# A fused six-layer decoder on one core: the step order of four compute engines is laid out anew

## What is computed

```python
x = LN(x + causal_self_attention(LN'(x)) + x)          # one head of 256, float32
x = LN(x + long_convolution(x, k, skip, ctx, ctx))      # 16 heads of 8, via FFT in the reference
x = LN(x + ternary_ffn(x))                              # hidden 1024, quantised to 8 bits, tanh for silu
x = LN(x + recurrence(x))                               # r, k, v, decayed cumulative sum, group norm
x = LN(x + cross_attention(x, ctx, mask))               # 16 heads of 128, 4 key/value heads
x = LN(x + gated_ffn_fp8(x))                            # gelu(x Wg) * (x Wu), then W
```

## Time and profile before

| what | us |
|---|---|
| median of 3 runs | 877.9 |
| lowest and highest | 875.35 and 879.66 |
| the profiled execution, its own time | 880.54 |
| its span, first to last instruction | 877.6 |
| busy: PE, PEld, DVE, ACT, POOL | 818.2, 639.2, 673.0, 522.4, 334.2 |

### The profile page before, as it was taken

One profiled execution on the slowest core, in us unless ns is written; L12 is line 12 of the kernel. 1 busy time (PEld: TensorE's weight loads), 2 busy tenths in 40 slices (PEclk: granted clock), 3 DMA queues, 4 the chain that ended last, 5 costly groups with the idle time before them and its releaser, 6 DMA issues.

```text
span 877.6 us, 14510 instructions
## 1 busy us (share of the span) xinstructions
PE 818.2 (93%) x5004; PEld 639.2 (73%) x5004; DVE 673.0 (77%) x1592; ACT 522.4 (60%) x1299; POOL 334.2 (38%) x419
## 2 busy tenths in 40 slices
PE   6877978999999999999999999999999999999984
PEld 5654856888786778777787777866788767787763
DVE  2696786888898869886897879986897789546554
ACT  4546126546636776387644975279634779568763
POOL 1453724533554336421762244713373244212100
PEclk9898989999999999999999999999999999999998
DMA  8942010010001000100001000010000000000000
GB/s 289 372 128 96 13 37 13 1 25 13 1 1 25 25 13 2 25 13 13 13 5 33 1 13 13 2 36 1 13 1 13 1 1 1 13 1 1 13 1 24
DMA packets 37064, 28.66 MB, mean 33 GB/s; under 512 B 18688, under 2 KB 34560, under 8 KB 36608
## 3 DMA queue, kind: packets, MB, share of 16 engines
q1 hardware_dynamic: 36992, 27.74, 10.3%
HBM read 25.64 MB, written 2.10 MB: 32 GB/s over the span
## 4 chain that ended last, share of the span: by engine, by line
PE 66%; DVE 19%; ACT 7%; issue 3%; POOL 3%; DMA 1%; POOLq 0%; DVEq 0%; SPq 0%; ACTq 0%
PE bank L1322 9%; PE bank L1361 9%; PE bank L1049 5%; PE bank L1340 5%; PE bank L1350 5%; PE bank L1240 5%; PE bank L1120 2%; PE bank L1345 2%; PE bank L1118 2%; PE bank L1121 2%; PE bank L1150 2%; PE bank L1188 2%; PE bank L1043 2%; DVE S L977 1%; PE bank L1068 1%
## 5 line engine op out<-in xcount | busy, mean ns | idle before, releaser
L1322 PE MATMUL bank<-XTE,w_xq 128*128 128x256 f32 x512 | 122.0, 381 | 0.8 <-ACT QA L670 0.8
L678 ACT ACTIVATE S<-S,mx 128x128 f32<-128x128 f32 x256 | 99.4, 395 | 37.9 <-DVE mx L980 37.4
L1361 PE MATMUL bank<-w_xo,OX 128*128 128x256 f32 x512 | 116.0, 380 | 0.0
L1322 PEld LDWEIGHTS bank<-XTE,w_xq 128*128 128x128 f32 x512 | 94.6, 191 | 17.4 <-issue 5.0
L1361 PEld LDWEIGHTS bank<-w_xo,OX 128*128 128x128 f32 x512 | 95.9, 190 | 15.5 <-issue 2.8
L669 ACT ACTIVATE QS<-bank,per_partition_sb 128x256 f32<-128x256 f32 x128 | 60.6, 473 | 53.1 <-PE bank L1322 47.4
L977 DVE SCALAR_TENSOR_TENSOR S<-bank,rq,xmask 128x128 f32<-128x128 f32 x256 | 71.5, 342 | 17.1 <-PE bank L1340 12.5
L1340 PEld LDWEIGHTS bank<-KTX,QA 128*128 128x128 f32 x512 | 63.8, 192 | 9.8 <-issue 7.5
L1340 PE MATMUL bank<-KTX,QA 128*128 128x128 f32 x512 | 67.9, 277 | 0.2 <-ACT OX L690 0.2
L289 POOL TENSOR_TENSOR prod<-XTA,ccolA 128x256 f32<-128x256 f32 x96 | 59.6, 652 | 22.1 <-PE bank L1121 15.8
L1350 PE MATMUL bank<-PT,VX 128*128 128x512 f32 x128 | 67.2, 610 | 0.2 <-ACT PT L685 0.2
(11 more groups left out here) (223 smaller groups left out, 1878.0 us busy)
## 6 DMA issues: line engine op xcount, KB each, us to landing
xin<-in_x SPq DMA_DIRECT2D x8, 256.0 KB, 2.7
taps_sb<-in_taps SPq DMA_DIRECT2D x1, 2048.0 KB, 11.7
...
w_xq<-in_L_xattn_Wq SPq DMA_DIRECT2D x1, 2048.0 KB, 12.1
...
```

What stands on the lines that cost most here:

```text
L678: ins = nc.scalar.activation(S[:, b, seq(h)], S[:, b, seq(h)], ACT.Exp, bias=mx[:, b, h:h + 1], accum_out=sm[:, b, h:h + 1])
L1322: ins = nc.tensor.matmul(cols(EQ)[:, h], w_xq[:, k, hh * XDIM:(hh + 1) * XDIM], XTE[:, k], start=k == 0, stop=k == HALVES - 1)
L1361: ins = nc.tensor.matmul(rows(EY)[:, b], OX[:, h, b], w_xo[:, n * XGROUP + h], start=n == 0 and h == 0 and b == 0, stop=n == XKV - 1 and h ...
```

## The change

The strings of `ORDER` for TensorE, VectorE, ScalarE and GpSimd are other ones. Each letter occurs as often as before, so each station issues the same instructions in the same sequence; only their interleaving differs. The string of SyncE, and with it the queue of DMAs, is the same. The first line of each changed string:

```diff
     "pe": (
-        "sassasaaasaaaaasaaqaaqasaqqqcqaccaccaqaaccccaaqaaraaraaaraqraqrqqrraacaqcqacqacxyqcqaqaqcaqaaqccaqac"
+        "asssasaasaaasaaaqaaaaaaaqaacqcacaqqscacqaqaaqaqacqaccaaacqarqrraraarcrcaarccqaqcqaaqyxcqaaqacaqcaqac"
...
     "act": (
-        "sassaasaasassssscqsqqcqacscaacccscaaccccarrrqqqqcaaacqacqacqcccqcaqcqccqycxyyccycxyxxyqxaqyxacaaaqyc"
+        "sassaasasasassssscaaacacacqqqccqaccscqsccqcqrqcraraacaacccqcaqcqccqcqcycxqqyccxyxcyaxayayaqayxqxcqyq"
...
```

More of the change, by code:

```diff
@@ L1378 @@
     "pe": (
-        "sassasaaasaaaaasaaqaaqasaqqqcqaccaccaqaaccccaaqaaraaraaaraqraqrqqrraacaqcqacqacxyqcqaqaqcaqaaqccaqac"
[L1380 to L1385, removed]
+        "asssasaasaaasaaaqaaaaaaaqaacqcacaqqscacqaqaaqaqacqaccaaacqarqrraraarcrcaarccqaqcqaaqyxcqaaqacaqcaqac"
+        "qyaqcxacycycxxaoycacayqyacxqxaqxoqyqycaqcaayqxcxaxcoacxqayaqyaxycacqcqcxaocqcacqcxyqcxcyaxqacqayqaqa"
+        "qoaqaxcayaqxcqyxqyoqacyqaqaxcyaxyaxcoqaayqyxaaxcqyxaaaoaccaycaqyacycxcacaqacqaxcaxyocqaayxqaqaqyxqxq"
+        "coqycxqycqaxqycqacqxayqoqyacqacxcqxcayaqxaaqaaqcaccaxcaoqcacqxyqaxqcyqayaqoaxqxcaycayxqcaaqaaoyqcqcx"
+        "yqaxyaaqyccaxocayxqyxcaqayaqxaaqoqcacaaaacqaxcqxcyaqcyqxyqcqoqxaxyqxcaqyaxcyaxqoaqcaqxyaaqycqyxocxqx"
+        "aqayaqxqayacycoaccxqaaqacaxcqcyaqcayqacyqcaaqcqyaqyoqaxyqxaqxcoqcxyqycqyxcaxocqyxaqyxcyqxoqyaqcyxqcy"
+        "axcqxoycaqcqcqcqyqcyacxqxayxcqoyqxyxaqxqoaxyqxyaqyoqxayqyaxqxyqaxoqaxyqxqyxayqaoxyqxayaxayaoaxyaxaya"
         "aoaaaaaaaaa"
@@ L1388 @@
     "dve": (
[L1389 to L1393, removed]
@@ L1394 @@
-        "xaqcaxcaqcoaqaoayqayaaxaaaxqcccaaacaycaacayacacaccqyaxyxcycqaxycxcccyaxyccqoaxqoaayqccqycxaxcqccycac"
-        "yacxcxcqyaxyaxaqyxyoxoaqayaxyxaqaaxyxayqaaxyaxyaaaaaooaaaaaaaaa"
+        "aasssasassaaasssaassaaaaasaaaaaaaaaaaqsaaacscqaqacacacaacqccqaaaasaccaaqacaaaaaaaaccaaacarcrrrararca"
+        "rcracacccqaaaccaaaayxayaqacaaacaacxaaacaaayqccyxccaxcyccayqcacaxaxcaycxcaxaqaacayacacccaayqaacaaacxq"
+        "caaxoyqoqccaccaccqxacaxcayacaacyaaaaqcyayxxcaaqcyaxaycxaacccaaacaaaaayaaoayqaaccaaacxaoxqacycacqacac"
@@ L1396 @@
+        "yaqcaxacxcqaccayxayxacaqcycycccqaxccxaaqcaaayqacaaaqcaaaxqxcaaaayaacaccocaqacoacaxyacxccayacaaaxqaac"
+        "aaycxyacccccayqxayxaaaaacayqacyqaacxqaoaqxaaaaaaoacaacacaccqcxcycxcycaxaxaycaaaqyxcaaxycaqayaxccxcqa"
+        "ccaayqaocacqaacaaqxayocxcaqaaacaacacyacyaaaacacaccqyxyxacqcycxayxcccacyqxcyxqoqaaqyccaoxycqcxcccycyc"
+        "xaacxcaqyxxyaaqyoyxaxaqayaxyxqoxayaxyaqaaxyaaxyaaaaoaoaaaaaaaaa"
     ),
     "act": (
-        "sassaasaasassssscqsqqcqacscaacccscaaccccarrrqqqqcaaacqacqacqcccqcaqcqccqycxyyccycxyxxyqxaqyxacaaaqyc"
@@ new lines @@
+        "cyaxcqxcxccxyccqxyycqcxccxcyccqxyxqaayxqaqacqaaqyaaqxcqyxcyqyqcaxqyacaxacyaxyxcqaycqyxcxcyccyycxcacx"
+        "ayaaxaaqyxqaacqyxqxqcqyxqcxyqycaqcxcyqacqycacaxqcacqxycaxyccxcxqqxyqqyaqxqcayxaqcaxycaaqaacyxcqcyqcy"
+        "xcaqycaaxcacayxxycqaxyqycxccqxqyxyqaqxqycxqxayqcaxqyaxcaayqcxaaqyxqycxcyxcqaxqaccayaayccxcaxcqycxqyc"
+        "qyqyqqyqcyqxaxaqycxqcyxqyccxcyaxcqycxcyqxyaxcyacaycxqxyqcxcayqqcqyaqxyxyqxqyxxqyxaqayxqyxyaqayxqyxaa"
+        "xqyxqxyxaqyaxyqxyaxyaaxayaaxayaxyaaaaaaa"
@@ L1404 @@
     ),
     "pool": (
-        "sassaaaaaaqaqcaccaacaqaaqararcarcaqacaqaaacqcaaccqcaacqaacaaoqcqcqaqcccaqaqcaaaacaaqcaoqcqcqccaqacqa"
-        "acaqaqaaqcqoaccccqaaqccaqcaoqcaqaaacqcacqcaaqcaqacaoqaqaacqccacqqccqoqcqcqaccqqoqqaqaoa"
+        "sassaaaaaaacaqqaacaacqaqacacarrarcaacqaaqacacaqcccqaaaacqcaqacoqcqacccqaqacaqacaaaoaqcacqcqccqaaqccq"
+        "aaacaqqacqacoqaccqaaccaqaaacqqaocaqacccqqacqacaqaoacqaqcaqaccacqcqcqoqqcqccacqqqqoaqaoa"
     ),
```

## The result

The changed kernel takes 879.57 us in the median of 20 runs (878.40 to 883.18), the kernel before 876.25 us (872.03 to 880.39, 20 runs beside it). The ratio is 1.0035, 95% interval 1.0019 to 1.0050: 3.3 us slower, forecast were 3. The runs of the kernel before differ by the mean granted clock of TensorE in the run: in the largest set beside an experiment, 22 of 35 had 0.984 to 0.988 and took 872.4 to 876.5 us, 13 had 0.980 and took 879.1 to 881.1; in other sets some lie between, at 0.981 to 0.983. The profiled execution of before (880.54 us, 0.980) is one of the upper group, and that of the change took 881.11 us (0.982), 1.5 above its median. The two profiles are therefore only 1.4 us apart in span (877.6 and 879.0). The runs of the changed kernel have 0.979 to 0.985, with no gap between them.

A forecast was written before the change was run, and what follows sets the result against it. The prediction took TensorE to bound the kernel wherever engines overlap, and chains through the other engines elsewhere. Start -3, middle +5 and end +1 gave +3 on the profiled 880.5 us, or 881 us against the median, range 868 to 892.

The forecast's parts named there:

- The start, -3: From 0 to 165 us: shorter waits and new waits sum to -2.6, say 3 us faster, with bounds of -15 and +4.
- L1043 behind the down product: In the start, the transposes of the normed rows lose the other work ahead of them and wait for the norm: +3.7 us.
- the second hidden block: In the start, two hidden blocks of group 1 stand back to back; the second waits for tanh and VectorE: +2.2 us.
- the wait behind the recurrence: In the start, the recurrence's rows are transposed 1.7 us of PE work after the output product, where it was 5.2: +2.5 us.
- The -9: In the start, more PE work covers the chain ahead of group 0's transposes of Q (L1195): 9 us gained, at least 5.
- the -4: In the start, other work fills the recurrence's output product's wait for VectorE and may keep the clock up: 2 to 5 us gained.
- The middle, +5: From 165 to 840 us: dependent steps packed closer leave more waits with too little cover, +5 us, between 0 and +9.
- ahead of the squares: In the middle, waits from a projection's end to its squares: 20 instead of 4 with cover below 1.8 us, +2.7 us.
- behind single copies: In the middle, waits of 1.0 us behind one copy: 21 instead of 5 with too little cover, +2.1 us.
- The end, +1: Group 6's last hidden block follows an L1361 step, so its copy delays the table load and gelu: +1 us.
- A start that gains and keeps it: Rival: the start's charged waits fall on top of each other, so only the first costs; 868 us, chance 0.23.
- VectorE and GpSimd in each other's way: Rival: VectorE's scaling of H (L880), on the chain to L1195 in every group, gets longer; 889 us, chance 0.23.

The follow-up runs named there:

- e5: New order from 0 to 303 us, the old order after it, against the kernel before: ratio 1.0026 (1.0007 to 1.0045).
- e4: The changed kernel with ScalarE's two L512 behind L554 again and TensorE's two L1032 moved back: 878.94 us, 1.0021 against the kernel before.
- part 1: The stretch from 0 to 303 us, ending where both orders have done the same steps; new order there alone: 1.0026 against the kernel before.
- e11: The kernel before with 50 dummy matmuls ahead of the L1049 of NT in group 0: 878.17 us, 1.0015 (0.9995 to 1.0035) against it.
- e10: The changed kernel with 130 instead of 60 dummy matmuls behind group 0's L1127: 879.39 us, 1.0036 against the kernel before.
- e12: Old order up to 603 us, new order from there, against the kernel before: 874.91 against 876.49 us, 0.9982 (0.9966 to 0.9999).
- part 2: The stretch from 303 to 603 us, cut where both orders have done the same steps; new order there alone: 1.0033 against the kernel before.
- part 3: The stretch from 603 to 852 us, cut where both orders have done the same steps; new order there alone: 0.9997 against the kernel before.
- Parts 3 and 4: The stretches from 603 to 852 us and from 852 us on; new order in each alone: 0.9997 and 0.9995 against the kernel before.

## Why the forecast was right, and where not

The forecast of 881.0 us, +3 us and inside half a percent, came out. Its three terms did not, and that they add up to the measured difference is luck: the start came out some 5 us dearer than forecast, the middle 3.4 and the end 1 us cheaper.

**The start, -3: the step that failed.** It is +2.1 us in the mean of the profiled executions, and the run e5 has +2.3 (0.6 to 3.9). By the prediction's own sign (wrong if PE's loss of the start rises) this term is refuted. Both waits that were to go are gone: L1195 waits nowhere in the first 165 us, and L1049 with NT takes 1.99 us behind no wait. The give-backs are there too: L1043 behind the down product 3.0 (forecast 3.7), and the second hidden block 3.7, under which the wait behind the recurrence falls (forecast 2.2 + 2.5). The two L880 of group 0 take 0.9 and 1.2 us (forecast: 2 us more in all; before they took 1.45 and 0.75). L554 begins at 27.27 (27), with 4.7 us at L1032; by e4 this cost 0.6 us (medians) to 1.4 (trace), where 0 was said. Not seen were L1043 for Z with 4.7 and L1118 with 2.1; L1043 waits 10.4 us for VectorE in all, where 6 were said.

What was wrong above all is the clock in the gains. The -9 added to a stall of 6.2 us the 2.5 us of low clock around it, and the -4 did the same with 1.8 us at L1049: 4.3 us in all, to come back with the waits. Over part 1 the low clock cost 0.8 us more with the new order, not 4.3 less. e11 shows one way in which such time gets lost: the 1.79 us that L1049 got back came again as the next wait, as the chain behind it is bound elsewhere. It is not the only way it can go, since e10's trace kept most of what it got back. The second fault is a term that the start did not have: the 1.8 us of busy time that no clock explains, of the kind that the prediction priced in the middle only. Idle time alone came out better than said: by the terms it should have grown by some 2 us (8.2 of stalls gone, 10.4 given back), and it fell by 0.4. Where in part 1 the 1.8 us lie is open.

There is a third fault, in what the term was read from. That was one execution of before, which belongs to the upper group. The old order ends part 1 some 3 us earlier in the mean, so the change's start had to beat 300.2, not 303.5. The sum corrected for the 2.6 us between the execution and the median, but the term took the low clock as something the new order would cure. The clock of 0.91, 0.92 and 0.74 in the earlier trace rows is only in part the order's: e12, with the same order here, has 1.00 up to 40 us and 0.95 up to 165. The Trainium skill, page "TensorE: Matmul & The Clock Gate", section "Part 1: The HAM clock gate", says that the unit that judges activity runs freely and not from the kernel's start, so that the same kernel loses a different amount in each run. The executions of part 1 agree that the amount differs, with 258.8 to 265.3 us for the same 1656 matmul instructions; that this is the reason, no run here shows.

**The middle, +5: a loss came, but smaller and not where it was put.** The busy time grew by 1.7 us in part 2 and 2.3 in part 3, 4.0 together against 4.8 in the working. The working put 2.7 of its 4.8 ahead of the squares (L1328) and 2.1 behind single copies. TensorE in part 2, first before, then the change:

```profile
L1322 PE MATMUL bank<-XTE,w_xq 128*128 128x256 f32 x200 | 47.4, 380 | 0.0
L1328 PE MATMUL bank<-QS,ones 128*32 128x256 f32 x96 | 7.7, 391 | 0.0
```

```profile
L1322 PE MATMUL bank<-XTE,w_xq 128*128 128x256 f32 x200 | 47.9, 382 | 0.5 <-issue 0.2 <-DVE KX L958 0.2
L1328 PE MATMUL bank<-QS,ones 128*32 128x256 f32 x96 | 7.7, 391 | 0.0
```

L1328 is as it was, and from start to start its matmuls lose 0.1 us more than before, those of L1270 another 0.1. The growth lies ahead of L1322 (+1.6), L1164 (+1.4), L1361 (+1.2), L1188 and L1340 (+1.0 each), and L1350, L1118 and the output product lose about 1 us less each. So the kind of loss was right, but not the places and with them not the prices. The working had also left out that the new order covers waits that were open before: idle falls by 2.8 us in part 3 and rises by 0.4 in part 2. Net +1.6. The sign in "what would show it" was wrong for the same reasons: the window from 165 to 840 us has 2.9 us less idle time, where 3 to 9 more were said. Too short a cover need not appear as idle time.

**The end, +1: nothing.** The last stretch is 1.5 us longer, but by the low clock inside L1150, which before paid earlier. Parts 3 and 4 take 272.8 against 273.2 us. Of the gelu's delay nothing is left to see.

Together +2.1 + 2.0 - 0.4 = +3.7 by the profiled executions, where the runs have 3.3 (1.7 to 4.4). The first of these terms is the mean of executions that lie up to 7 us apart, so it could be a microsecond off, and no closer agreement should be read into it.

**The rivals.** A start that gains and keeps it (868 us) is refuted by e5. VectorE and GpSimd in each other's way (889 us) went the other way, and the profile shows the price of one such meeting. On GpSimd, then on VectorE, kernel before:

```profile
523.09 2.37 POOL L452 TENSOR_TENSOR H<-H,g 128x1024 f32<-128x1024 f32 x1 [7.12 <-ACT Q L603]
```

```profile
523.17 2.84 DVE L880 TENSOR_SCALAR H<-H,fac 128x1024 f32<-128x1024 f32 x1
```

L880 ends 0.55 us after L452 has ended. In before six of its 16 lie under an L452 for 1.7 us or more and take 2.25 to 2.84 us, and a seventh with 0.9 us of overlap takes 1.45; with the change a single one does, with 2.25. By the Trainium skill, page "SBUF — State Buffer", section "SBUF: two separate sides", whichever of the two starts first holds the shared ports for its whole instruction; the rows agree for L452. Beside GpSimd's L398 an L880 takes 0.74 us, as if alone. So the change took 8.6 us of L880 from VectorE (23.1 to 14.5), and no gain from it can be seen in the time. That PE's work covers it is likely and not shown, since no run changed L880 alone.
